# Counting edges per lane on VectorE instead of TensorE in the edge layer of a graph network kernel

## The reference, cut to what matters

```python
out_deg  = segment_sum(ones, src, num_segments=n)
norm_src = rsqrt(maximum(out_deg, 1.0))
```

## Time and profile before

| | |
|---|---|
| device time, median of 3 runs | 16642.69 us (16616.44 to 16654.34) |
| profiled execution | span 16655.4 us |
| busy PE / PEld / DVE / ACT / POOL | 45 / 32 / 48 / 36 / 44% |
| edge stage, gather batches 753 to 7297 us | 6544 us of the span |

### The profile page before, as it was taken

The page is one execution under the profiler, slowest core; times in us unless marked ns, Lnnn a source line. Parts: engine busy times, 40 slices in busy tenths (PEclk is TensorE's granted clock), DMA queues, the critical chain, the costliest instruction groups (busy, mean ns, idle before and its releaser), DMA issues. The chain is left out here.

```text
span 16655.4 us, 228031 instructions
## 1 busy us (share of the span) xinstructions
PE 7442.4 (45%) x71916; PEld 5270.8 (32%) x71916; DVE 8010.3 (48%) x11391; ACT 6068.0 (36%) x10705; POOL 7332.9 (44%) x7085
## 2 busy tenths in 40 slices
PE   1244444454444544446988999960000000000055
PEld 1133333343333433333544555530000000000045
DVE  4255555555555555555444434444444444444475
ACT  0132323333333333335777777742222222222200
POOL 4444444444444544433111111136666666666610
PEclk9855555655655555568999989965555555555587
DMA  6333333333333333335655656632222222222186
GB/s 265 131 97 109 98 109 97 110 107 99 109 97 110 110 97 110 98 102 147 203 174 175 204 155 204 204 112 57 58 56 55 57 58 56 57 55 58 48 290 225
DMA packets 1622965, 1983.45 MB, mean 119 GB/s; under 512 B 513957, under 2 KB 1419270, under 8 KB 1617497
## 3 DMA queue, kind: packets, MB, share of 16 engines
q1 hardware_dynamic: 1302057, 1257.39, 25.7%
q10 hardware_dynamic: 94032, 435.46, 6.4%
q0 software_dynamic: 226176, 281.93, 6.1%
HBM read 1171.70 MB, written 816.17 MB: 119 GB/s over the span
## 5 line engine op out<-in xcount | busy, mean ns | idle before, releaser
L645 POOL DMA_INDIRECT RF<-tab_edge_b,idx x3125 | 3236.0, 1036 | 3666.1 <-DMA idx<-e_src 2659.8
L1208 POOL DMA_INDIRECT records<-RF,idx x3125 | 3092.0, 989 | 1597.5 <-issue 990.9
L698 DVE TENSOR_TENSOR HM<-iota_b,eqw 128x2048 bf16<-128x2048 bf16 x2000 | 2192.1, 1097 | 2833.1 <-remote 1632.3
L1969 PE MATMUL bk<-HM 128*128 128x98 bf16 x16000 | 1637.7, 257 | 3164.9 <-issue 1606.4
L1809 ACT ACTIVATE X<-bk 128x392 uint8<-128x392 f32 x4000 | 1808.6, 495 | 2479.3 <-remote 1340.3
L1969 PEld LDWEIGHTS bk<-HM 128*128 128x128 bf16 x16000 | 1152.0, 120 | 3647.1 <-issue 3558.5
L1969 PE MATMUL kp<-HM,ident_b 128*128 128x98 bf16 x3125 | 275.2, 282 | 4380.6 <-DVEq L1718 2422.7
L782 PE MATMUL tp<-HM,RF 128*64 128x512 bf16 x12276 | 2003.6, 379 | 6.1 <-DVE HM L743 1.1
L882 POOL DMA_INDIRECT agg<-RF,lastT x372 | 528.3, 1420 | 2864.9 <-ACT RF L821 2774.1
L1969 PEld LDWEIGHTS kp<-HM,ident_b 128*128 128x128 bf16 x3125 | 251.6, 142 | 4405.1 <-issue 4405.1
L788 PE MATMUL om<-HM,RF 128*64 128x512 bf16 x6138 | 1451.4, 379 | 0.0
(11 more groups left out here) (376 smaller groups left out, 14562.8 us busy)
## 6 DMA issues: line engine op xcount, KB each, us to landing
dst_f<-counts SPq DMA_DIRECT2D x465, 512.0 KB
RF<-first_rows SPq DMA_DIRECT2D x250, 800.0 KB
counts<-X ACTq DMA_DIRECT2D x250, 784.0 KB
RF<-records SPq DMA_DIRECT2D x220, 784.0 KB, 5.2
records<-pivots SPq DMA_DIRECT2D x120, 1400.0 KB
crow<-counts SPq DMA_DIRECT2D x279, 512.0 KB
first_rows<-RF ACTq DMA_DIRECT2D x25, 4000.0 KB
edge_rows<-RF ACTq DMA_DIRECT2D x125, 800.0 KB
```

The costliest lines, as they stand in the source:

```text
L645: e.indirect_dma_start(out=ring[:, r, j, :], out_offset=None, in_=table[:, :], in_offset=bass.IndirectOffsetOnAxis(ap=idx[:, r, own(j):own ...
L698: return e.tensor_tensor(to[:, 0:n, :].rearrange("p k (q h) -> p k q h", h=2), iota_b[:, 0:m].rearrange("p (q h) -> p q h", h=2).unsqueeze ...
L1208: e.indirect_dma_start(out=records[:, :], out_offset=bass.IndirectOffsetOnAxis(ap=idx2[:, r, j:j + 1], axis=0), in_=msgs[MSG_OF[r]][:, j, ...
L1969: return e.matmul(to, by_q, by_r, start=start, stop=stop, skip_group_check=True)
```

## The change

The 25 products with `ident_b` per block go away, and with them `cnt` in PSUM, its clearing at the start and its copy at the end. VectorE sums the same `ohr` one-hots itself: a new helper `lane_counts` reduces the one-hots of a part over its 16 or 9 edges into `stat["tmp"]` and adds that to `stat["incl"]`, which is cleared ahead of the stage. It runs twice in a block: part 0 between the histogram's one-hots and pair v = 0 (which overwrites the buffer of part 0), part 1 between pair v = 0 and pair v = 1.

```diff
-        cnt = mixed[:, TILES + 2 * P:2 * TILES + 2 * P]
...
-            chain(e.memset(cnt, 0.0))
...
+            def lane_counts(b, h):
+                n = len(HIST[h])
+                wait(e, "batched", b * (VB + 2) + (h + 1))
+                gate(e)
+                loop_chain(e.tensor_reduce(out=stat["tmp"][:, :], in_=ohr[h][:, 0:n, :].rearrange("p k q -> p q k"), op=ALU.add, axis=AX.X))
+                loop_chain(e.tensor_tensor(stat["incl"][:, :], stat["incl"][:, :], stat["tmp"][:, :], ALU.add))
...
                 for h in range(2):
                     for _ in hist_batch(b, h):
                         several(filling, 1)
+                lane_counts(b, 0)
                 for _ in count_batch(b, r, 0):
                     several(filling, 1)
+                lane_counts(b, 1)
                 taking = max_steps(b, r)
...
+            chain(e.memset(stat["incl"][:, :], 0.0))
             chain(e.memset(zero_cols, 0.0))
...
-            chain(e.tensor_copy(stat["incl"][:, :], cnt))
...
                 for c in range(len(HIST[h])):
                     first = isinstance(b, int) and b + h + c == 0
-                    whole(hist, ohq[h][:, c, :], ohr[h][:, c, :], first, c == len(HIST[h]) - 1)
-                    last = whole(cnt, ident_b[:, :], ohr[h][:, c, :], False, c == len(HIST[h]) - 1)
+                    last = whole(hist, ohq[h][:, c, :], ohr[h][:, c, :], first, c == len(HIST[h]) - 1)
                 last.then_inc(sem("histed"), 1)
```

## The result

| | before | after |
|---|---|---|
| device time, median of 4 runs each | 16632.49 us | 15999.95 us (15993.63 to 16003.64) |
| ratio, 95% interval | | 0.9625 [0.9609, 0.964] |
| profiled span | 16655.4 us | 16001.9 us |

The account below looks back on a forecast made before the run. No engine was full; the order of waits bounded the edge stage, with TensorE's results reaching others late during gathers. 2.0 us x 119 intervals = 240 us off 16655 gave 16415, forecast 16400 us, range 16070 to 16760.

Parts of the forecast that it names:

- pair v = 3: Sign on VectorE: this one-hot pair, 37.5 us after the gathers' start before, would start before the gathers end or right behind.
- Rival 1: Edge stage: stalls belong to the gathers alone, so nothing is gained and the addition is covered; 16640 us, chance 0.17 with rival 4.
- rival 4: TensorE's counting products were free, being hidden in a stage where TensorE isn't full; same time as rival 1, joint chance 0.17.
- the sum: Edge stage: three ordinary blocks in five 3.36 us shorter, 2.0 us an interval, times 119: 240 us less.
- The strong form: Edge stage: all blocks become like the early 50.15 us interval, 576 us less, 16067 us; chance 0.15.
- early interval of 50.15: Short gather interval from 753.53 in the kernel before, histogram done 6.2 us after the gathers' start; taken as the strong form's model.
- the former is already the better kind, and the latter has its own stall: Last written-out block (52.99 us) and loop's turn (mean 57.1 us) were left unchanged, with no gain counted.
- The histogram on TensorE: 25 of 50 products removed at 81 ns each: 2.0 us a block instead of 4.0.
- The reduces: VectorE's two new reduces per block at the contiguous price: 1.79 us for part 0, 1.07 for part 1.
- In an ordinary block the addition costs nothing: VectorE's added 4.1 us a block fit the cover, 7.42 us idle ahead of pair v = 3; uncovered they cost 490 us.
- Gathers: GpSimd's gathers under VectorE's added instructions: taken as 0, with up to 0.4 us a batch, 44 us in all, in the range.
- Rival 3: VectorE becomes the bound in every block once the 7.42 us of cover are used up: at most 290 us, 16930; chance 0.13.

Follow-up runs that it names:

- removal alone: Kernel before without the 25 products, counts made on VectorE after the edge stage: with stalls 16725.53 us (1.0034), interval 48.49 us; without stalls 14401.92 us (1.0686).
- fourth group: Four runs on one chip with stalls: before 17027.44 us, changed kernel 16528.49, part 0 on VectorE with part 1 on TensorE 16937.57, changed kernel with 18 semaphore increments 16805.45.
- the pass: Separate VectorE counting after the edge stage, added to the kernel before without its 25 products: 124 steps of 6.92 us, 865 us in all.
- counts later: Changed kernel with own buffers for the histogram's one-hots, reduces moved behind pairs v = 3 and v = 4: 16423.5 us, ratio 0.9674 to before, with stalls.
- addition alone: Changed kernel with the 25 products put back, so both engines count: 17026.2 us (1.0021 to before) with stalls, 13771.14 us (1.0221) without.
- the late products: Kernel before with its 25 products moved to the block's end (sums unread), counts made after the stage: 17300.5 us with stalls, 1.037 to before.
- padding: Changed kernel with 18 semaphore increments on TensorE at the end of each block: 16805.45 us, ratio 0.9886 to before, with stalls.

## Why the prediction was right and wrong

**Right.** The direction, and the mechanism in outline. The gain comes by the interval alone (650 of 653 us of span), by TensorE's earlier end of the histogram, through ScalarE's second copy of turned rows and the first banks, to VectorE's pair v = 3, which starts under the gathers, as the prediction asked. Rival 1 with rival 4 is refuted where the stalls are: the interval fell by 5.5 us, and with removal alone by 6.4. The removal carries it. Without the stalls rival 4 holds: there the products were free.

**The step that failed: the sum.** The forecast took 51.57 us for an ordinary interval, and left the last block and the turn as they were. All three terms were mis-sized: ordinary blocks came at 48.4 to 49.0, worth (6.19 + 6.42 + 5.83) / 5 x 119 = 439 us instead of 240; the last block fell by 4.83, 115 us; the turn by 4.04, 96 us; together 650. The strong form was nearest (16067, and the range ended at 16070, 70 us above the time), and even the early interval of 50.15 was no floor, since that block still had its 50 products. The reasoning "the former is already the better kind, and the latter has its own stall" was wrong: the lateness is in each of them, and the same 25 products are ahead of each (in the kernel before, the second copy of turned rows stands at 12.6 us in the last block too, by the median, 12.6 to 13.0 in the ordinary ones, and 23.7 at the turn). The forecast also had 240 us for the removal and nothing for the addition; on one chip these are 757 and 140 us, so two errors of opposite sign make up the 616.

**Why the size was off.** The forecast read the lateness as growing with what is queued, by a proportion: half way between two blocks. The runs show something steeper. In the fourth group the interval moves by 0.2 us from 50 products to 34 (56.02 to 55.79), and from 34 to 25 by another 3.6, though a second reduce is added there. A price per product can't be read from a trace that has one number of them only. What was at hand and not followed is the way from the first bank to pair v = 3. The argument stopped at the first bank. The timeline of ACT in the same block of the kernel before goes on:

```profile
6050.00 0.50 ACT L1809 ACTIVATE X<-bk 128x392 uint8<-128x392 f32 x1 [4.42 <-remote]
6054.90 0.50 ACT L1809 ACTIVATE X<-bk 128x392 uint8<-128x392 f32 x1 [4.40 <-remote]
6060.57 0.60 ACT L1825 ACTIVATE hT<-tp 128x512 f32<-128x512 f32 x1 [5.17 <-remote]
```

From the first bank (6043.65) to the fourth (6054.90) it took 11.25 us, and 3.51 in the kernel after: 7.7 us, more than twice the 3.4 by which the first bank itself came earlier (16.0 to 12.6). The waits on "remote" come again behind the first bank, up to 5.2 us each while the gathers run, and the change took most of that away.

**The histogram on TensorE** was forecast to take 2.0 us less. Its 25 products run from 6006.31 to 6009.01, 2.7 us instead of 4.04, since TensorE now waits 0.54 us for part 1 of the one-hots. The second transposes came 1.2 us earlier instead of 2.0, at 6.2 us, the very place of the early interval. That 1.2 us went with 5.5 us of the interval. The 81 ns a product of the forecast is the distance of their starts; the distance of their answers, under the stalls, is two to three times that (see the last section).

**The reduces.** Forecast 1.79 and 1.07 us at the contiguous price, "with a step of 98 elements, which no row shows". Measured 2.84 and 1.74 us, 1.81 and 1.98 ns an element; over 25 x 98 in the pass 4.40 us, 1.80 an element, where the earlier trace rows have 2.71 for as many contiguous ones. With adds and idles the parts hold VectorE for 3.4 us (6008.49 to 6011.88) and 2.3 us (6014.31 to 6016.57), 5.7 instead of 4.1, and pair v = 0 is 1.7 us late and pair v = 1 3.5, instead of 0.7 and 1.9. The Trainium skill (VectorE: DVE Perf Modes, "The perf-mode tier table") gives this reduce one element a cycle; the contiguous rows agreed, these do not, and the measurement decides.

**"In an ordinary block the addition costs nothing."** It costs 1.18 us an interval where the stalls are (49.67 against 48.49), a fifth of what it holds VectorE for. The first bank goes from 9.4 to 12.6 with it, but counts later has it at 9.4 and is no faster, so that this is the reason isn't shown. The cover was the stall itself, and it shrank with the stall: ahead of pair v = 3 VectorE idles 2.70 us in the block shown, where it was 7.42.

**Gathers.** Forecast 0 to 0.4 us a batch, measured (1094 - 1036) x 25 = 1.45. But it is not the reduces: removal alone, without them in the block, has 1087 ns, and addition alone, with both and its stalls, 1046. The gathers are slower where VectorE gets more of its other work done under them. That reduces don't slow them agrees with the page named in the prediction (the Trainium skill, SBUF — State Buffer, "Who interferes with whom"), by which a reduce never takes the port pair that VectorE shares with GpSimd.

**Rival 3** did not decide in the measured comparison, and did decide, as a mechanism, in the other condition: VectorE at 92%, 1.0206. Its price was put at no more than 290 us, and the measured loss is 282; that they are so near is chance, since the price was worked out for intervals of 55 us. The reduces cost more than the prediction knew, and with the interval at 37 us there is no cover.

**Open.** What makes TensorE answer more slowly while the gathers run, why the interval goes by the products ahead with such a steep step between 34 and 25, and what sets the condition itself. A run that would put only the histogram's end back met the other condition.

## What to carry to other kernels

When a stage is paced by waits that end on nothing in the record, the worth of removed work can't be had from its duration: 2.0 us of products gave 6.4 us an interval, 16 of the 25 gave 0.2. Take out the least piece and time it before you forecast by proportion, and don't exempt any kind of block from the sum. Price a reduce by its stride (here 1.8 to 2.0 ns an element against 1.1), and ask for each move of work to VectorE what happens when the stalls that cover it are gone: this one is worth -2.8 to -3.8% with them and +2.1% without.

## What the runs showed of the hardware that was not expected

The same program has two conditions 3,150 to 3,540 us apart. The kernel before took 16,599 to 17,051 us beside the changed kernel's first run and in three groups, and 13,453 to 13,502 in two; one chip was in the faster condition first and in the slower later, another the other way round, so it is no property of the chip. In the slower condition the waits of ScalarE's copies of turned rows on "remote" come to 955 to 1850 us with 34 or more products in the histogram, to 200 to 364 with 25, to 700 with 25 and the late products, and to 1070 with 25 and padding; in the faster one no large wait is on "remote". The condition isn't confined to the edge stage: of the 2,249 us between the two profiled executions of the changed kernel (16001.9 and 13752.6), the 119 intervals make 1,479, and the rest lies before and behind them. Gathers take no longer in the slower condition (1029 to 1094 ns against 1112 to 1146), so they are not its cause. The granted clock of the stage is somewhat lower (0.57 against 0.63 in the changed kernel), but TensorE starts the histogram's products 82 ns apart in both (addition alone).

The traces' semaphore events say what "remote" stands for. In the kernel before, TensorE raises the semaphore of the second transposes 4.3 us after the last of them has started (medians over 66 blocks off the loop's turn), in the kernel after 0.5 us; in addition alone it is 5.3 us with the stalls and 0.35 without. Between the semaphores of the histogram's part 0 and part 1 lie 18 products, in the kernel before as in addition alone. They are answered 1.5 us apart without the stalls (82 ns a product), 3.0 us apart in the kernel before (164 ns) and 4.4 us in addition alone with the stalls (246 ns). So the answers aren't late by a fixed time. They come at a lower rate than the starts, and a backlog grows from the histogram on, which the kernel after doesn't have there: it has 0.3 us behind part 0 and 0.5 behind part 1. By these rates 25 products are 4.1 to 6.2 us of backlog and not 2.0, an estimate, which is near the 5.5 to 6.4 us that the interval lost; no run shows that the one makes the other. Whether TensorE computes more slowly or only its semaphores are held up, and what sets the condition, the runs don't show.
